# Opening of an attention block: where the second group's weight fold and a modulation step stand in the order of work

## The reference

```python
mod = (_silu(L0_c) @ L0_wmod).reshape(L0_c.shape[0], 6, 1, -1)
sa, ca, ga, sb, cb, gb = (mod[:, 0], mod[:, 1], mod[:, 2], mod[:, 3], mod[:, 4], mod[:, 5])
ga = (2 * (ga >= 0) - 1) * jnp.maximum(jnp.abs(ga), 0.25)
gb = (2 * (gb >= 0) - 1) * jnp.maximum(jnp.abs(gb), 0.25)
h = _layernorm(x, axis=-1) * (1 + ca) + sa
x = x + ga * attention(h, wq_a, q_a_ln_w, wq_b, wkv_a, kv_a_ln_w, wkv_b, wo)
h = _layernorm(x, axis=-1) * (1 + cb) + sb
x = x + gb * feed_forward(h)          # int8 weights, 512 -> 1376 -> 512, silu gate
```

```python
q = _rmsnorm(x @ wq_a.T, q_a_ln_w) @ wq_b.T          # per head 64 plain + 64 rotary
ckv_kpe = x @ wkv_a.T                                # 32 latents + 64 rotary, shared by all heads
kv = _rmsnorm(ckv, kv_a_ln_w) @ wkv_b.T              # per head 64 key + 128 value
q_pe = _apply_rope(_deinterleave(q_pe), cos, sin)
k_pe = _apply_rope(_deinterleave(k_pe), cos, sin)
scores = jnp.einsum('bqhd,bkhd->bhqk', q_full, k_full) * softmax_scale
attn = jax.nn.softmax(jnp.where(causal, scores, min), axis=-1)
out = jnp.einsum('bhqk,bkhd->bqhd', attn, v).reshape(B, S, H * VD) @ wo.T
```

## Time and profile before

| | us |
|---|---|
| median of 3 runs | 720.97 |
| the 3 runs | 719.98, 720.97, 726.5 |
| profiled execution, own time | 720.49 |
| its span | 718.7 |
| TensorE busy in it | 684.4 |
| VectorE busy | 526.6 |
| ScalarE busy | 288.4 |
| GpSimd busy | 258.9 |

### The profile page before, as it was taken

How to read it: one execution, slowest core, us unless ns; L and a number is a source line. 1 busy time by engine, 2 the same in 40 slices (tenths; PEclk the granted TensorE clock), 3 DMA queues, 4 the chain that set the end, 5 groups by cost and what they waited for, 6 DMA issues and landing times.

```text
span 718.7 us, 9328 instructions
## 1 busy us (share of the span) xinstructions
PE 684.4 (95%) x3539; PEld 486.7 (68%) x3539; DVE 526.6 (73%) x762; ACT 288.4 (40%) x427; POOL 258.9 (36%) x164
## 2 busy tenths in 40 slices
PE   2989899999999999999999999899999999999997
PEld 1854477666676675665675665456888888887886
DVE  6878689989999999899899796796882331323432
ACT  4742344534544545445345343352444322322120
POOL 2137622934745645546538204213651000000111
PEclk9999999999999999999999999999999999999999
DMA  8935533303404304313332803810211413100101
GB/s 318 280 90 133 134 77 88 92 17 89 107 1 108 88 8 102 88 41 81 74 81 60 301 2 111 299 59 6 83 29 41 135 46 88 47 1 1 44 31 44
DMA packets 40972, 63.34 MB, mean 88 GB/s; under 512 B 5536, under 2 KB 21664, under 8 KB 39072
## 3 DMA queue, kind: packets, MB, share of 16 engines
q1 hardware_dynamic: 40928, 62.75, 32.0%
HBM read 32.99 MB, written 2.10 MB: 49 GB/s over the span
## 4 chain that ended last, share of the span: by engine, by line
PE 62%; DVE 14%; POOL 8%; DMA 8%; issue 3%; ACT 2%; SPq 2%; DVEq 0%; ACTq 0%; POOLq 0%
PE PS L975 17%; PE PS L992 8%; PE PS L798 7%; DMA Q<-TQ 5%; PE PS L861 5%; PE PS L939 5%; PE PS L868 5%; PE PS L864 5%; PE PS L879 4%; DVE MX L1423 3%; POOL RT L1738 3%; POOL RT L1737 3%; POOL TQ L1776 2%; DVE PR L1518 2%; SPq L562 2%
## 5 line engine op out<-in xcount | busy, mean ns | idle before, releaser
L1423 DVE TRANSPOSE_TENSOR_REDUCE MX<-PS 128x16 f32<-128x512 f32 x288 | 182.5, 686 | 24.3 <-PE PS L798 23.2
L1167 ACT ACTIVATE PR<-PS 128x1024 f32<-128x1024 f32 x108 | 99.5, 929 | 128.7 <-PE PS L868 90.3
L861 PE MATMUL PS<-Q,KH 96*128 96x512 f32 x288 | 118.9, 413 | 4.2 <-ACT PR L1167 2.8
L868 PE MATMUL PS<-Q,KH 97*128 97x512 f32 (+1 forms) x288 | 114.5, 397 | 0.2 <-DMA Q<-NM 0.2
L864 PE MATMUL PS<-Q,KL 96*128 96x512 f32 (+1 forms) x288 | 113.9, 395 | 0.0
L798 PE MATMUL PS<-Q,KH 96*128 96x512 f32 (+1 forms) x288 | 103.4, 422 | 3.9 <-DMA Q<-TQ 2.4
L861 PEld LDWEIGHTS PS<-Q,KH 96*128 96x128 f32 x288 | 54.8, 190 | 40.5 <-ACT PR L1167 16.9
L798 PEld LDWEIGHTS PS<-Q,KH 96*128 96x128 f32 (+1 forms) x288 | 53.0, 191 | 28.1 <-issue 13.4
L1518 DVE TENSOR_TENSOR PR<-PR 128x2048 f32<-128x2048 f32 (+1 forms) x28 | 69.3, 2476 | 0.2
L1645 DVE SCALAR_TENSOR_TENSOR wide<-PS,ffn_s,TQ 128x1024 f32<-128x1024 f32 x10 | 12.8, 1284 | 72.6 <-PE PS L975 72.6
L1167 ACT ACTIVATE wide<-PS 128x1024 f32<-128x1024 f32 (+1 forms) x48 | 45.7, 953 | 50.3 <-PE PS L868 44.2
(11 more groups left out here) (196 smaller groups left out, 1101.3 us busy)
## 6 DMA issues: line engine op xcount, KB each, us to landing
Q<-TQ SPq DMA_DIRECT2D x56, 384.0 KB, 6.5
RT<-in_wo SPq DMA_DIRECT2D x4, 1024.0 KB, 5.5
TQ<-in_wo SPq DMA_DIRECT2D x4, 1024.0 KB, 6.8
Q<-TQ SPq DMA_DIRECT2D x16, 192.0 KB, 3.4
WI<-in_gate_w SPq DMA_DIRECT2D x10, 256.0 KB, 3.3
WI<-in_up_w SPq DMA_DIRECT2D x10, 256.0 KB, 3.9
DI<-in_down_w SPq DMA_DIRECT2D x10, 256.0 KB, 2.7
PR<-in_wmod_c SPq DMA_DIRECT2D x2, 1024.0 KB, 6.3
```

What stands on the lines that cost most here:

```text
L861: pe.matmul(dst, M.KH[0:KR, ks], M.Q[0:KR, w % 2, 0, qb, :, qs], start=True, stop=False)
L868: ins = pe.matmul(dst, M.KH[0:rows, ks], M.Q[0:rows, w % 2, 1, qb, :, qs], start=False, stop=True)
L1167: act.activation(tiles, banks, ACT.Exp).then_inc(S_.p, 1)
L1423: dve.tensor_reduce(M.MX[:, kt, qt // 4, :, qt % 4, :], PS[:, bank_of(turn), :].rearrange("p (h s q) -> p h s q", h=HG, q=L), axis=AX.X, o ...
```

## The change

Three places of the order are changed, on all engines alike. The fold of group 1, `("w", 1)`, moves from ahead of `("split", 0, 1)` to behind part 2 of the maxima. The step of the gates' products that stood ahead of part 0 moves behind part 4, and the other steps are laid out anew: behind parts 4, 8, 13, 18, 22 and 27 instead of ahead of part 0 and behind 6, 12, 17, 21 and 25; the first gate's copy moves from part 8 to part 9. `("even", 1, 0)` moves from part 3 to part 5. At the end, `("low", 1, 1)` moves from between `("join", 0)` and `("rows", 0)` to behind `("rows", 0)`.

As `keep_busy` leaves out odd keys of `MOD_PIECES`, the pairs behind parts 9, 13 and 27 go and those behind 17, 21 and 25 come in. Banks 3, 4 and 6 change hands in the opening: bank 4's last user before window 0 is part 35 instead of `("lat", 1, 1)`, which has bank 6.

```diff
 FIRST_QUERIES[1].remove(("low", 0, 1))
-FIRST_QUERIES[1].insert(3, ("w", 1))
...
-FIRST_MAXIMA = MOD_STEPS[2:3]
-MOD_PIECES = dict(zip((6, 12, 17, 21, 25), ([step] for step in MOD_STEPS[3:])))
-MOD_PIECES.update({8: [("modrow", 0, 0)], 30: [("modrow", 0, 1)]})
+FIRST_MAXIMA = []
+MOD_PIECES = dict(zip((4, 8, 13, 18, 22, 27), ([step] for step in MOD_STEPS[2:])))
+MOD_PIECES[9] = [("modrow", 0, 0)]
+MOD_PIECES[30] = [("modrow", 0, 1)]
+MOD_PIECES[2] = [("w", 1)]
...
-HANDED_PIECES = {3: [("even", 1, 0)], 7: [("odd", 1, 0)], 11: [("lat", 1, 0), ("sum", 1, 0)], 14: [("split", 1, 0)],
+HANDED_PIECES = {5: [("even", 1, 0)], 7: [("odd", 1, 0)], 11: [("lat", 1, 0), ("sum", 1, 0)], 14: [("split", 1, 0)],
                  22: [("even", 1, 1)], 26: [("odd", 1, 1)], 29: [("sum", 1, 1)]}
...
-FIRST_MAXIMA.insert(FIRST_MAXIMA.index(("join", 0)) + 1, ("low", 1, 1))
-FIRST_MAXIMA.append(("split", 1, 1))
+FIRST_MAXIMA += [("low", 1, 1), ("split", 1, 1)]
```

## The result

The changed kernel takes 724.53 us (median of 13 runs, 722.99 to 728.61); the kernel before, in the same series, 721.07. The ratio is 1.0046 with an interval of 1.0027 to 1.0065: slower by 3.5 us, inside the one per cent. The forecast was 724.4. It rests on a stall that came where it was put, and on two smaller items that went another way and cancel in part.

The account below looks back on a forecast made before the run. TensorE, busy 95% of the span, was taken as the bound, delays of window 0 reaching the end one to one. Maxima +2.0, row -0.1, clock +1.5 made +3.4 us: 724.4 against the median, range 721.0 to 727.5.

Parts of the forecast that it names:

- a stall: TensorE waits 3.1 us before ("even", 1, 0) for GpSimd's low rest of the folded weights.
- two smaller items: After the opening: group 1's later DMAs stay hidden at no cost, and the low clock at 88 stays.
- Step 1: Opening: TensorE's first parts start 1.4 us earlier, worth nothing because part 10 waits for the DMA landing at 60.97.
- Step 2: Fold's copies queue behind ("split", 0, 1) on ScalarE and GpSimd; ("even", 1, 0) goes at 58.85 after 3.1 us of waiting.
- Step 3: Parts behind the stall: the maxima end 1.9 to 2.0 us later at full clock, bounds 1.1 and 3.1.
- Step 4: Row of maxima: its reduction goes first, 0.1 us won; group 1's DMAs come about 0.7 later but stay hidden.
- hidden, with 0.7 to spare: DMAs of group 1's second query half land by 95.0, before part 10 of group 1 reads at 96.41.
- Step 5: Clock behind the stall: one low stretch of 3.2 us at 1.2 GHz, costing 1.5 us.
- The upper length of the prediction: A longer low stretch of the clock behind the stall, 6.8 us, would lose 3.1 us.
- The sum: Maxima 2.0 later, row 0.1 earlier, clock 1.5: +3.4 us, 724.4 against the median.
- rival C: Not slower: the low stretch at 88, start of window 0, is gone, -1.5 us; 721.4 in all; chance 0.13.
- Forecast A: Opening: the stall and one low clock stretch behind it, 724.4 us; chance 0.45.

Follow-up runs that it names:

- e2_fold_back: The changed kernel with the fold ("w", 1) put back ahead of ("split", 0, 1): 721.58 us, ratio 1.0005.
- e3_copies_first: The changed kernel, but ScalarE and GpSimd take their share of ("w", 1) ahead of ("split", 0, 1): 722.55 us, ratio 1.0012.
- e1_fold_alone: The kernel before with only the fold ("w", 1) moved behind part 2: 725.20 us, ratio 1.0053.
- e4_busy_stall: The changed kernel with 13 idle bf16 matmuls ahead of ("even", 1, 0): 723.42 us, ratio 1.0025.
- e5_low_alone: The kernel before with only ("low", 1, 1) moved behind ("rows", 0): 721.62 us, ratio 1.0011.
- e6_low_back: The changed kernel with ("low", 1, 1) put back between join and rows: 724.90 us, ratio 1.0049.
- e7_steps_alone: The kernel before with only the steps of the gates' products laid out as changed: 722.16 us, ratio 1.0010.
- e9_latents_earlier: The kernel before with group 2's weights loaded early, ("lat", 1, 1) behind part 31 and ("low", 1, 1) behind part 33: 720.38 us, ratio 0.9995.
- e10: The changed kernel with ("even", 1, 0) behind part 9 and ("odd", 1, 0) behind part 10: 723.58 us, ratio 1.0041.
- e8_weights_first: The kernel before with group 2's weights loaded ahead of the sends of group 1's first query half: 720.19 us, ratio 0.9989.

## Why the prediction was right

- Step 1, the head start: 1.4 us forecast, keep_busy starts 1.55 earlier. That it is worth nothing is shown by e2_fold_back and e3_copies_first, where it turned into waits of 1.50 and 1.98 us for the DMA instead of the 0.56 of before.
- Step 2: forecast copies at 55.2, low rest 57.7 to 58.7, product at 58.85 after 3.1 us of waiting. Measured, net of the axis: 55.2, 57.67 to 58.67, 58.82, and 3.29. The cause is shown by undoing it (e2_fold_back), by doing it alone (e1_fold_alone), and by changing only the two engines' order (e3_copies_first).
- Step 3, the maxima 2.0 later at full clock: 1.7 in e4_busy_stall, which has the stall's length and no low stretch. The term was 0.3 too large. VectorE's waits at parts 23 and 28, forecast from the pairs of keep_busy that come back, are in the profile of the changed kernel as 0.80 and 0.38 us. (The 0.27 of before stood at part 27, not at 28 as the prediction reads it: part 15 is the first of the twelve.)
- Step 4: the row's reduction starts 0.33 after the transpose instead of 0.46, so 0.13 won (0.1 forecast). The other half of the step failed: "hidden, with 0.7 to spare". The wait is 0.83 us, and 0.95 in e5_low_alone. The fault was to measure the slack against part 10 of group 1 at 96.41, a time that itself held the low stretch of 88 to 91. Without that stretch the reader comes 1.5 earlier and the slack is spent, so the added lateness of 0.7 becomes a wait. What it costs in the end is less sure: 0.6 in e5_low_alone, but undoing it in e6_low_back gave back only 0.1 at equal clock, four runs against four.
- Step 5: one low stretch, 1.5 us. Measured 3.4 us long, 1.6 us in price (e4_busy_stall). The upper length of the prediction, 6.8 us, stands in no row of the kernel before; the changed kernel has one of 6.9, at 463. What makes a wait bring one is not settled: 1.98 us did in e3_copies_first, and 2.40 in the kernel before did not. The prediction set that row against the rule of the Trainium skill (TensorE: Matmul & The Clock Gate, section "Why this matters for your kernels"); the rule speaks only of gaps longer than that, so the row doesn't contradict it. The 1.98 us are shorter than the rule's gaps, too, and a low stretch followed them.
- The sum: 724.4 against 724.53. Part of this is luck. In the profile the low stretch at 88 disappeared, as rival C had it (-1.5), the late DMAs took 0.8 of that back, and this execution gained a low stretch elsewhere. At equal clock the change costs 1.7 to 1.9, and the median has one low stretch more than before; that this one is always the stall's isn't shown. Forecast A holds for the opening up to the row (+3.2 against 3.4); for the rest of the time it is A with half of C. The low stretch at 463, 370 us behind the last edit, is not the change's own: all twelve profiles have the wait for that DMA, and six have a low stretch at it, among them e2_fold_back, e7_steps_alone and e9_latents_earlier, which have no stall of 3 us. Whether it comes more often in the changed kernel is open.

## What to carry to other kernels

Moving a piece of work in a list that several engines share moves it on each of them, and the engine that the edit has in mind is often not the one that pays: look for the engines that did their share in a wait, and where that share lands in their queue. A head start ahead of a transfer was worth nothing here, and the work that filled the wait for it cost its full time once it was behind. And measure slack against the reader's time without its own accidents (a low clock), not as the one trace has it.

## What the runs showed of the hardware

The granted clock explains most of the scatter between executions of one program: at 1.000, 0.998 and 0.995 the kernel before takes 719.96, 721.40 and 722.91 us, each group within 0.9 of its mean but for the last (1.2). Which idle time is followed by a low stretch isn't told by the length of the one wait. TensorE's wait for the output weights near 460 (us, one profile each, by the first letters of the run's name) shows it best, as every kernel has it:

```
followed by a low stretch    1.84 (e2)  2.45 (e7)  2.58 (e1)  2.63 (e6)  2.70 (changed)  2.73 (e9)
clock stayed full            1.93 (e4)  1.93 (e5)  2.21 (e10)  2.40 (before)  2.62 (e8)  2.69 (e3)
```

So the time of an edit of a microsecond in the opening can come out more than a microsecond higher or lower by the clock alone. The median of e8_weights_first is lower by the clock and not at equal clock; e9_latents_earlier gained at equal clock, and the clock took part of it back.
